# Attention and mixture-of-experts kernel on one core: the output projection as three fp32r products, with one normed macro tile, one probability buffer and five routing groups at the end

## The chip, the core and the metric

The kernel runs on one core of a Trainium2 chip. The metric is the device time of one execution in microseconds (us). A profiled execution comes with a trace; a span is the time from its first to its last instruction. The engines are named as the profile names them: PE is TensorE (matrix products; PEld is its loading of weights), DVE is VectorE, ACT is ScalarE, POOL is GpSimd, and SP issues most of the DMAs.

## What is computed

64 sequences of 64 tokens and 256 features go through a conditioned low-rank adapter, attention with a sink logit, and a mixture of 32 experts of which each token takes 4. Cut to what matters (`h` is the head count 16 on 4 key/value heads):

```python
def reference(x, cond, ...):
    x0 = relu(x @ (w_down * dg + db)) @ (w_up * ug + ub) + x     # per sequence
    qkv = rmsnorm(x0, attn_norm_w) @ qkv_w + qkv_b               # q: 16x64, k, v: 4x64
    q, k = rope(q), rope(k)
    logits = causal(q @ k.T / 8)
    attn = exp(logits - logaddexp(logsumexp(logits), sink))
    y = attn @ v                                                 # 1024 wide
    x2 = x0 + (y @ proj_w + proj_b)                              # the output projection
    h2 = rmsnorm(x2, ffn_norm_w)
    topv, topi = top_k(h2 @ gate_w + gate_b, 4); gw = softmax(topv)
    y2 = sum over the 4 experts e of gw_e * (silu(h2 @ Wg_e) * (h2 @ Wu_e)) @ Wd_e
    return x + x2 + y2
```

## The kernel before, in words

**Two parts.** The 4096 tokens are 8 macro tiles of 512 tokens (index m), each of 4 tiles of 128 tokens (index t, 0 to 31). Part one, the first 520 us or so, does adapter, attention, projection and routing. Part two runs some 159 expert tiles of 128 listed tokens each, then adds the four rows of every token. The change is in part one.

**Order.** Every engine runs a list of steps written out by hand in `ORDERS`: a start, a first period, a period that is repeated for each macro tile, and an end. The period of m does the attention and projection of macro tile m's tiles and, interleaved, the norm and the query/key products (`pair`, five of them) of macro tile m + 1. An engine waits at a step until semaphores say that its inputs and its output buffer are ready; steps behind it on that engine wait too.

**The chain of one tile.** `score` (PE) makes the logits in PSUM; `softmax_a` (DVE: a row maximum, L1497, and a subtraction, L1499), an exponential on ACT, and `softmax_b` (DVE: a sum, L1505, a reciprocal and the normed probabilities `prob`, L1516) follow; `turn_prob` (PE, L873) transposes them and ACT copies them out; `attend` (PE, L888) makes y in two PSUM banks; ACT copies y to `y_t` (L1186, two instructions per tile); `project` (PE) adds x0 and the product of `y_t` and `w_o` in one PSUM bank (L903); DVE adds the bias and writes `x2` (L1526). The product is in plain fp32: 8 products of 128 x 128 x 256 per tile, which the trace shows as 16 instructions.

**The norm of the next macro tile.** `sums` (PE, L811), two ACT instructions, `apply` (DVE: L1465 multiplies, ACT takes the upper part, L1469 subtracts it for the lower part). The two parts, `h_t`, feed the fp32r products of `pair` (PE, L822) and `value` (L834, six products each). An fp32r product here is three: upper by upper, upper by lower, lower by upper. `pair`'s results go through DVE (L1482, four of 128x512 per pair) and POOL (L708, L710), and are moved to `q_r` and `k_r` by DMAs that SP issues.

**Routing.** A group of tiles (`ROOTS`) is routed together: `route_turn` for each of its tiles (PE, ACT), `route_pick` (PE logits, DVE L1535 to L1563: the four best experts), `route_count` (PE, DVE), `route_list` (DVE L1583 to L1602: the slots). Then ACT packs and tags the rows (`pack`, `tag`) and POOL writes them to the experts' lists (`put`, L719, four indirect DMAs per tile). Before, the groups are the macro tiles 0 to 6 whole, and the last one as 2, 1 and 1 tiles: ten groups. When the last put has landed, ACT loads list rows (L1324) and part two begins, if the plan of expert tiles that DVE makes from the last counts (to L1710) is ready.

**Weights.** Between these steps each expert matrix is loaded, split by ACT (`split`, L1241) and POOL (L726) into two parts, and stored to `w_parts`.

## Time and profile before

| | |
|---|---|
| Times of three runs | 986.27, 989.08, 989.81 us; median 989.08 us |
| The profiled execution | 986.29 us, span 984.4 us |
| PE busy | 883.4 us (90%), 7248 instructions |
| PEld busy | 730.9 us (74%) |
| DVE busy | 793.0 us (81%), 1795 instructions |
| ACT busy | 523.8 us (53%) |
| POOL busy | 544.6 us (55%) |

The page's shares are means over both parts. For part one the stretches must be read apart: by the eight `apply` steps (L1465), which start at 31.4 us and then every 57 to 59 us from 78.7 to 426.8 us. A stretch's row gives the busy time of each engine in it. A busy PE is not PE at its peak, since the ends of its instructions are modelled and neighbours overlap; DVE's are as they ran.

### The profile page before, as it was taken

Reading aid. Unit: us, or ns where it says so; the run is one execution under the profiler, and the core shown is the slowest. Engines: PE = TensorE matmul, PEld = TensorE weight load, DVE = VectorE, ACT = ScalarE, POOL = GpSimd, SP = SyncE. Lnnn points to the kernel's source line nnn. Section 1 sums busy time; section 2 is a strip of 40 time slices with the busy share of each in tenths; the row PEclk is TensorE's granted clock in tenths of the full one; section 3 lists DMA queues with packets and bytes.
Section 4 is the critical chain, followed back from the end, with each engine's and each line's share of the span. In section 5 each row is a group of like instructions: output and inputs, shape, how many; then the busy total and the mean of one; then the engine's idle time right before and its main releaser. Section 6 shows DMA issues by size and latency. Waiting matters only on the chain.

```text
span 984.4 us, 21528 instructions
## 1 busy us (share of the span) xinstructions
PE 883.4 (90%) x7248; PEld 730.9 (74%) x7280; DVE 793.0 (81%) x1795; ACT 523.8 (53%) x1241; POOL 544.6 (55%) x507
## 2 busy tenths in 40 slices
PE   3759899898989989898981899999999999999998
PEld 1537677676767768676760688888888888888887
DVE  5888699899989989897764577777777787777777
ACT  3134464645647464563660466666666666666641
POOL 3455668888788888888357133343433333433340
PEclk8879999999999999999895799999999999999999
DMA  8388999888897988979239777877777758663698
GB/s 287 91 248 278 299 299 266 267 279 256 271 289 253 303 271 279 279 243 286 104 108 369 233 255 250 295 247 257 251 249 273 266 192 301 243 231 106 247 394 302
DMA packets 127446, 251.39 MB, mean 255 GB/s; under 512 B 18756, under 2 KB 66122, under 8 KB 126797
## 3 DMA queue, kind: packets, MB, share of 16 engines
q1 hardware_dynamic: 83436, 186.79, 57.4%
q0 software_dynamic: 13776, 34.64, 9.6%
q10 hardware_dynamic: 30128, 28.58, 9.4%
q8 instruction: 63, 1.03, 0.5%
q14 instruction: 43, 0.34, 0.1%
HBM read 135.64 MB, written 102.12 MB: 242 GB/s over the span
## 4 chain that ended last, share of the span: by engine, by line
PE 59%; DVE 11%; POOL 10%; issue 7%; DMA 6%; ACT 4%; SPq 2%; ACTq 0%; DVEq 0%; POOLq 0%
PE scores L1031 11%; PE gbank L1031 11%; PE scores L1050 6%; PE gbank L1050 5%; PE gbank L903 5%; POOL lists L719 4%; PE gbank L822 3%; DMA w_parts<-ring 3%; DVE ring L1482 3%; POOL ring L726 3%; PE gbank L1094 2%; PE scores L1005 2%; PE gbank L1005 2%; PE gbank L1040 2%; PE scores L1040 2%
## 5 line engine op out<-in xcount | busy, mean ns | idle before, releaser
L741 POOL DMA_INDIRECT pick_rows<-rows_out,pair_i x159 | 158.6, 998 | 261.8 <-ACT rows_out L1306 258.3
L726 POOL TENSOR_TENSOR ring<-ring 128x512 fp32r<-128x512 f32 x96 | 125.3, 1319 | 84.1 <-ACT ring L1241 83.9
L1031 PE MATMUL scores<-ring,in_part 128*128 x480 | 133.3, 414 | 1.2 <-DVE in_part L1722 1.2
L1031 PE MATMUL gbank<-ring,in_part 128*128 x474 | 129.8, 409 | 0.0
L822 PE MATMUL gbank<-h_t,w_qk 128*128 128x512 f32 x480 | 119.2, 403 | 4.2 <-issue 3.8
L719 POOL DMA_INDIRECT lists<-put_rows,slot_i x104 | 101.3, 974 | 34.0 <-issue 28.5
L903 PE MATMUL gbank<-w_o,ring 128*128 128x256 f32 x512 | 118.1, 385 | 1.3 <-ACT ring L1186 1.1
L1241 ACT ACTIVATE ring<-ring 128x512 fp32r<-128x512 f32 x96 | 58.9, 627 | 113.1 <-DMA w_parts<-ring 65.0
L1482 DVE SCALAR_TENSOR_TENSOR ring<-gbank,b_qk,rope 128x512 f32<-128x512 f32 x160 | 108.6, 743 | 6.6 <-PE gbank L822 4.2
L822 PEld LDWEIGHTS gbank<-h_t,w_qk 128*128 128x128 f32 x480 | 89.6, 191 | 28.4 <-issue 7.7
L903 PEld LDWEIGHTS gbank<-w_o,ring 128*128 128x128 f32 x512 | 96.2, 193 | 14.5 <-ACT ring L1186 2.6
L1031 PEld LDWEIGHTS scores<-ring,in_part 128*128 128x128 f32 x480 | 85.6, 192 | 15.9 <-issue 1.6
L1031 PEld LDWEIGHTS gbank<-ring,in_part 128*128 128x128 f32 x474 | 83.3, 189 | 13.7
L1050 PEld LDWEIGHTS scores<-ring,mid_part 128*128 128x128 f32 x480 | 67.8, 189 | 7.7 <-issue 0.4
L1050 PEld LDWEIGHTS gbank<-ring,mid_part 128*128 128x128 f32 x474 | 67.0, 189 | 7.2
L1292 ACT ACTIVATE in_part<-scores,norm_w 128x128 fp32r<-128x128 f32 x160 | 50.0, 364 | 39.5 <-PE scores L1005 22.0
L1050 PE MATMUL scores<-ring,mid_part 128*128 x480 | 70.1, 282 | 0.1
L1050 PE MATMUL gbank<-ring,mid_part 128*128 x474 | 69.2, 282 | 0.0
L1730 DVE SCALAR_TENSOR_TENSOR mid<-scores,rows_in,silu 128x256 f32<-128x256 f32 x80 | 38.6, 483 | 35.6 <-ACT silu L1298 35.6
L1298 ACT ACTIVATE silu<-scores,rows_in 128x256 f32<-128x256 f32 x80 | 37.9, 473 | 51.7 <-PE scores L1031 51.7
L1730 DVE SCALAR_TENSOR_TENSOR mid<-gbank,rows_in,silu 128x256 f32<-128x256 f32 x79 | 38.1, 482 | 27.0 <-ACT silu L1298 27.0
L1298 ACT ACTIVATE silu<-gbank,rows_in 128x256 f32<-128x256 f32 x79 | 37.4, 473 | 41.7 <-PE gbank L1031 40.8
(210 smaller groups left out, 1864.0 us busy)
## 6 DMA issues: line engine op xcount, KB each, us to landing
w_parts<-ring SPq DMA_DIRECT2D x192, 256.0 KB, 3.8
ring<-w_parts SPq DMA_DIRECT2D x32, 1536.0 KB, 7.7
rows_in<-lists ACTq DMA_DIRECT2D x159, 136.0 KB, 3.9
ring<-in_W_up SPq DMA_DIRECT2D x64, 256.0 KB, 3.7
picks<-pick_rows SPq DMA_DIRECT2D x6, 2048.0 KB, 17.9
ring<-in_W_down SPq DMA_DIRECT2D x32, 256.0 KB, 4.7
q_r<-rot SPq DMA_DIRECT2D x16, 512.0 KB, 6.4
q_r<-ring SPq DMA_DIRECT2D x16, 512.0 KB, 5.9
```

What stands on the lines that cost most here:

```text
L719: e.indirect_dma_start(out=lists, out_offset=bass.IndirectOffsetOnAxis(ap=slot_i[r % NPAY][:, s * TOPK + k:s * TOPK + k + 1], axis=0), in_ ...
L726: e.tensor_tensor(lower, lower.bitcast(F32), upper.bitcast(F32), ALU.subtract).then_inc(s_lower, 1)
L741: e.indirect_dma_start(out=pick_rows, out_offset=bass.IndirectOffsetOnAxis(ap=pair_i[:, i:i + 1], axis=0), in_=rows_out[i % NY][:, :], in_ ...
L822: ins = e.matmul(bank[:, :], w_qk[:, x, c, 2 * j + o, :], h_t[i][:, y, c, :], start=k == 0, stop=k == len(CHUNK_PRODUCTS) - 1)
L903: ins = e.matmul(bank[:, 0:D], y_t[:, n // REP, n % REP, :, :].rearrange("p b s -> p (b s)"), w_o[:, n, :], start=False, stop=n == 2 * REP ...
L1031: ins = e.matmul(front[i % FRONTS], in_parts[i % IN_BUFS][x][:, c, :], ring[:, bass.ds(at + y * WE + c * 2 * DFF, 2 * DFF)], start=k == 0, ...
L1050: ins = e.matmul(out, mid_parts[i % 2][x][:, c, :], ring[:, bass.ds(at + y * WE + KC * 2 * DFF + c * D, D)], start=k == 0, stop=k == len(C ...
L1241: e.activation(w_upper[q % NU], w_third[q % NW].bitcast(F32), ACT.Copy).then_inc(s_upper, 1)
L1292: ins = e.activation(in_parts[i % IN_BUFS][0][:, c, :], front[i % FRONTS][:, c * P:(c + 1) * P], ACT.Copy, scale=norm2_w[:, c:c + 1])
L1298: e.activation(silu[i % 2][:, :], front[i % FRONTS][:, DFF:2 * DFF], ACT.Silu, scale=rows_in[i % NG][:, D + 2:D + 3]).then_inc(s_silu, 1)
L1482: e.scalar_tensor_tensor(out=by_seq(t[n][:, :]), in0=by_seq(gbank[banks[o]][:, :]), scalar=b_qk[:, 2 * j + o:2 * j + o + 1], in1=rope[:, t ...
L1730: e.scalar_tensor_tensor(out=mid[i % MID_BUFS][:, :], in0=front[i % FRONTS][:, 0:DFF], scalar=rows_in[i % NG][:, D + 2:D + 3], in1=silu[i ...
```

## The change

- **Projection.** `w_o` becomes two fp32r parts, `w_o[0]` (upper) and `w_o[1]` (lower). They are made once by a new step `outs` (two ACT copies and two DVE subtractions of 128x1024; the matrix is loaded into `x2` first). `y_t` becomes two fp32r tiles: ACT's copy writes the upper part, and a new DVE step `attend` subtracts it from PSUM for the lower part, two instructions of 128x512 per tile. `project` makes 24 fp32r products instead of 8 in fp32. The two PSUM banks of y are freed by the DVE step and no longer by the ACT copy.
- **Buffers.** To make room, `h_t` is one macro tile instead of two (with `act` inside it), `prob` is one buffer instead of two, `x2_t` lies in the ring of expert weights (so those loads wait for the last routing product), and `v_s` has five buffers instead of two, since all four `value` steps of a macro tile now come before the next `down`.
- **Routing.** The last two macro tiles are routed in five groups (2, 2, 2, 1 and 1 tiles) instead of four (4, 2, 1 and 1). The four extra put buffers go to tiles 26 to 29 instead of 24 to 27.
- **Order.** All lists in `ORDERS` are new. A third entry of `SUMS` that was always 0 is removed with its code.

```diff
-SUMS = [(3, 1, 0), (3, 1, 0), (2, 2, 0), (3, 1, 0), (2, 2, 0), (2, 2, 0), (2, 2, 0), (3, 1, 0)]
+SUMS = [(3, 1), (3, 1), (2, 2), (3, 1), (2, 2), (2, 2), (2, 2), (3, 1)]
...
-        softmax_a softmax_a value softmax_b apply project softmax_b pair pair route_pick pair value
-        softmax_a route_count project pair pair value route_list softmax_b value down project relu
+        softmax_a softmax_a softmax_b attend apply project softmax_b pair pair route_pick pair
+        attend softmax_a project route_count pair pair value value value route_list value attend
...
-ROOTS = [(m, 0, TPM) for m in range(NM - 1)] + [(NM - 1, 0, 2), (NM - 1, 2, 3), (NM - 1, 3, 4)]
+ROOTS = [(m, 0, TPM) for m in range(NM - 2)] + [(NM - 2, 0, 2), (NM - 2, 2, 4), (NM - 1, 0, 2), (NM - 1, 2, 3),
+                                                (NM - 1, 3, 4)]
...
-    w_o = sb1("w_o", [P, H * DH // P, D])
+    w_o = [sb1(f"w_o{h}", [P, H * DH // P, D], F32R) for h in range(2)]
...
-    h_t = [sb1(f"h_t{i}", [P, 2, KC, MT], F32R) for i in range(2)]
+    h_t = sb1("h_t", [P, 2, KC, MT], F32R)
+    act = h_t[:, 0, 0, :]
...
+    y_t = [sb1(f"y_t{h}", [P, 2, REP, 2, T], F32R) for h in range(2)]
+    x2_t = ring_space[:, (NW + NU) * THIRD:(NW + NU) * THIRD + KC * TPM * P].rearrange("p (c n) -> p c n", c=KC)
...
-    prob = [sb1(f"prob{i}", [P, 16, T]) for i in range(2)]
+    prob = sb1("prob", [P, 16, T])
...
         w.wait_ge(s_proj, NT)
+        w.wait_ge(s_gate, GROUPS)
         for n in range(1, RING):
             load_expert(n)
...
             for b in range(2):
-                freed[banks[b]] = (s_y, 2 * t + b + 1)
+                freed[banks[b]] = (s_y_lower, 2 * t + b + 1)
...
             w.wait_ge(s_y, 2 * t + 2)
-            for n in range(2 * REP):
-                ins = e.matmul(bank[:, 0:D], y_t[:, n // REP, n % REP, :, :].rearrange("p b s -> p (b s)"), w_o[:, n, :],
-                               start=False, stop=n == 2 * REP - 1, skip_group_check=True)
+            w.wait_ge(s_o_split, 2)
+            for x, y in ((0, 0), (0, 1), (1, 0)):
+                if x:
+                    w.wait_ge(s_y_lower, 2 * t + 2)
+                for n in range(2 * REP):
+                    ins = e.matmul(bank[:, 0:D], y_t[x][:, n // REP, n % REP, :, :].rearrange("p b s -> p (b s)"),
+                                   w_o[y][:, n, :], start=False, stop=x == 1 and n == 2 * REP - 1, skip_group_check=True)
...
+        def outs():
+            w.wait_ge(s_late, LATE)
+            for h in range(2):
+                at = slice(h * REP, (h + 1) * REP)
+                e.activation(w_o[0][:, at, :], x2[h][:, :, :], ACT.Copy).then_inc(s_o_upper, 1)
...
+        def outs():
+            for h in range(2):
+                at = slice(h * REP, (h + 1) * REP)
+                w.wait_ge(s_o_upper, h + 1)
+                e.tensor_tensor(w_o[1][:, at, :], x2[h][:, :, :], w_o[0][:, at, :].bitcast(F32),
+                                ALU.subtract).then_inc(s_o_split, 1)
+
+        def attend(t, banks):
+            if t:
+                w.wait_ge(s_proj, t)
+            for b in range(2):
+                w.wait_ge(s_y, 2 * t + b + 1)
+                e.tensor_tensor(y_t[1][:, :, :, b, :].rearrange("p g j s -> p (g j) s"),
+                                gbank[banks[b]][:, :].rearrange("p (c s) -> p c s", s=T),
+                                y_t[0][:, :, :, b, :].rearrange("p g j s -> p (g j) s").bitcast(F32),
+                                ALU.subtract).then_inc(s_y_lower, 1)
...
-            if t >= 2:
-                w.wait_ge(s_pt, 2 * t - 2)
+            if t:
+                w.wait_ge(s_pt, 2 * t)
```

In the rows below, `beside` and `stat` hold a tile's row maxima and sums, `gbank` are PSUM banks and `glog` the routing logits.

On DVE, at the start of a period, before: from the second tile's `softmax_b` to the first `pair`.

```order
L1505 TENSOR_REDUCE beside1<-scores 128x16
L1508 TENSOR_REDUCE stat1<-beside1 128x16
L1510 RECIPROCAL stat1<-stat1 128x16
L1516 TENSOR_TENSOR prob1<-scores,stat1 128x1024
L1465 TENSOR_TENSOR ring<-x0_t1,gbank0 128x512 x2
L1469 TENSOR_TENSOR h_t1<-ring,h_t1 128x512 x2
L1526 TENSOR_TENSOR x2_0<-gbank2,b_o 128x256
```

And now, at the same place on DVE:

```order
L1523 TENSOR_REDUCE beside1<-scores 128x16
L1526 TENSOR_REDUCE stat1<-beside1 128x16
L1528 RECIPROCAL stat1<-stat1 128x16
L1534 TENSOR_TENSOR prob<-scores,stat1 128x1024
L1446 TENSOR_TENSOR y_t1<-gbank1,y_t0 128x8x64
L1446 TENSOR_TENSOR y_t1<-gbank2,y_t0 128x8x64
L1483 TENSOR_TENSOR ring<-x0_t1,gbank0 128x512 x2
L1487 TENSOR_TENSOR h_t<-ring,h_t 128x512 x2
L1544 TENSOR_TENSOR x2_0<-gbank3,b_o 128x256
```

Two subtractions (L1446) stand in front of `apply`; the same two are added for each of the four tiles of a period.

On DVE, in the end section, before: from the second `softmax_a` of tiles 29 and 30 to the pick of tiles 24 to 27.

```order
L1499 SCALAR_TENSOR_TENSOR scores<-beside0,scores 128x1024
L1505 TENSOR_REDUCE beside1<-scores 128x16
L1508 TENSOR_REDUCE stat1<-beside1 128x16
L1510 RECIPROCAL stat1<-stat1 128x16
L1516 TENSOR_TENSOR prob1<-scores,stat1 128x1024
L1491 TENSOR_TENSOR v_s1<-gbank2,b_v 128x256
L1505 TENSOR_REDUCE beside0<-scores 128x16
L1508 TENSOR_REDUCE stat0<-beside0 128x16
L1510 RECIPROCAL stat0<-stat0 128x16
L1516 TENSOR_TENSOR prob0<-scores,stat0 128x1024
L1526 TENSOR_TENSOR x2_1<-gbank3,b_o 128x256
L1535 TENSOR_TENSOR glog<-gbank2,rms2_0 128x128
```

And now, on DVE from the same `softmax_a`:

```order
L1517 SCALAR_TENSOR_TENSOR scores<-beside0,scores 128x1024
L1560 SCALAR_TENSOR_TENSOR glog<-gbank2,rms2_0,b_gate 128x32 x2
L1566 MAX top<-glog 128x8 x2
L1569 MAX_INDEX top_i<-top,glog 128x8 x2
L1570 TENSOR_TENSOR gexp<-top 128x8
L1573 TENSOR_TENSOR onehot<-expert_no,top_i 128x256
L1581 TENSOR_REDUCE picked<-onehot 128x64
L1446 TENSOR_TENSOR y_t1<-gbank3,y_t0 128x8x64
L1446 TENSOR_TENSOR y_t1<-gbank0,y_t0 128x8x64
```

The pick of tiles 24 and 25 has moved in front of two `softmax_b` steps, a `value` and a `project`.

## Rows read from the trace of the kernel before

**Rows 1.** The page, part 4: the chain that ended last, shares of the span.

```profile
PE 59%; DVE 11%; POOL 10%; issue 7%; DMA 6%; ACT 4%; SPq 2%; ACTq 0%; DVEq 0%; POOLq 0%
```

**Rows 2.** Busy time by stretch: from:to, length, each engine (instructions), PE clock, DMA share, GB/s.

```profile
78.69:426.83 348.14, 319.20 (x3381) 248.08 (x3404) 316.69 (x511) 192.83 (x424) 277.77 (x238) 1.00 0.87 277
426.83:476.00 49.17, 43.96 (x385) 34.77 (x387) 40.00 (x71) 21.92 (x50) 37.60 (x33) 0.93 0.78 243
476.00:521.00 45.00, 36.38 (x473) 28.18 (x474) 33.43 (x96) 30.56 (x80) 21.82 (x24) 0.97 0.36 122
546.00:984.40 438.40, 434.10 (x2662) 386.54 (x2660) 338.77 (x989) 255.24 (x649) 158.63 (x159) 0.99 0.74 257
```

**Rows 3.** Waits of DVE, 78.69 to 426.83: us in total, times, longest.

```profile
DVE beside L1497 <- PE scores L860: 6.2, 4, 2.1
DVE act L1396 <- ACT act L1116: 5.2, 6, 1.6
DVE gbank L1383 <- PE gbank L790: 2.7, 1, 2.7
DVE beside L1497 <- issue: 2.2, 2, 1.1
DVE v_s L1491 <- PE gbank L834: 1.8, 5, 1.1
...
DVE h_t L1469 <- ACT h_t L1163: 0.3, 1, 0.3
```

**Rows 4.** DVE subtractions and products by line: duration in ns, least/median/most; and one pair of them.

```profile
L1465 DVE TENSOR_TENSOR ring<-x_t,gbank x14: 679/685/689, 78.7 to 427.4; 128x512 f32<-128x512 f32 x14
L1595 DVE TENSOR_TENSOR onehot<-onehot,rank x10: 285/682/1829, 165.4 to 523.6; 128x512 f32<-128x512 f32 x7, 128x128 f32<-128x128 f32 x2, 128x256 f32<-128x256 f32 x1
369.60 1.28 DVE L1465 TENSOR_TENSOR ring<-x_t,gbank 128x512 f32<-128x512 f32 x2
```

**Rows 5.** The chain that ended last in order of time: start, us, what.

```profile
442.60 0.71 PE gbank L834 x6
...
443.53 3.46 PE gbank L903 x16
...
463.69 2.65 issue
...
470.55 5.42 PE gbank L903 x16
```

**Rows 6.** Timeline of POOL, the last 32 puts: start, us, [idle before, releaser].

```profile
500.29 0.95 POOL L719 DMA_INDIRECT lists<-q_r,slot_i  x1 [16.47 <-ACT q_r L1233]
...
539.62 0.96 POOL L719 DMA_INDIRECT lists<-q_r,slot_i  x1 [0.30 <-issue]
```

**Rows 7.** Timeline of DVE and of ACT's queue, end of part one.

```profile
482.35 1.22 DVE L1505 TENSOR_REDUCE beside<-scores 128x16 f32<-128x1024 f32 x1
...
489.62 0.29 DVE L1535 TENSOR_TENSOR glog<-gbank,rms 128x128 f32<-128x128 f32 x1 [0.47 <-PE gbank L925]
...
498.37 0.17 DVE L1602 CAST slot_i<-slot_f 128x16 int32<-128x16 f32 x1
...
524.26 0.17 DVE L1602 CAST slot_i<-slot_f 128x4 int32<-128x4 f32 x1
...
533.83 0.41 DVE L1710 TENSOR_SCALAR ring_wait<-x_t 1x32 int32<-1x32 f32 x1
...
542.15 3.74 ACTq L1324 DMA_DIRECT2D rows_in<-lists  x6
```

**Rows 8.** Timeline of the start, where `outs` goes.

```profile
26.00 2.88 DVE L1430 TENSOR_TENSOR w_qk<-q_r,w_qk 128x1280 fp32r<-128x1280 f32 x2
...
30.07 0.66 ACT L1154 ACTIVATE gbank<-gbank,eps 128x512 f32<-128x512 f32 x1 [3.33 <-PE gbank L811]
...
36.90 13.47 DVE L1482 SCALAR_TENSOR_TENSOR ring<-gbank,b_qk,rope 128x512 f32<-128x512 f32 x19 [2.52 <-PE gbank L822]
```

**Rows 9.** Busy time by stretch, just after the wait at 463.69 (columns as in rows 2).

```profile
466.00:476.00 10.00, 9.08 (x98) 6.71 (x100) 5.34 (x6) 3.79 (x9) 4.82 (x6) 0.66 0.51 186
```

More of the change, by code:

```diff
@@ L74 @@
     "PE": ("""
[L75 removed]
+        cond down up sums pair pair pair pair pair value value value value down score up
     """, """
[L77 to L79 removed]
+        score turn_prob sums attend score project pair pair turn_prob score attend pair project pair
@@ L89 @@
+        route_count turn_prob attend score route_pick project route_turn turn_prob route_count
+        route_turn route_pick attend project turn_prob route_count route_turn attend route_pick
+        project route_count route_turn route_pick route_count
     """),
     "DVE": ("""
-        cond down relu scale up weights apply pair pair pair pair pair constants down relu softmax_a
-        up softmax_b value
+        cond down relu scale up weights apply outs pair pair pair pair pair value value constants
@@ L93 @@
+        down value relu value softmax_a up softmax_b
     """, """
-        value softmax_a softmax_b apply project softmax_a pair pair softmax_a value pair softmax_b
-        project value pair pair softmax_b down relu project value softmax_a up softmax_b project
+        softmax_a softmax_b attend apply project softmax_a pair pair softmax_a attend pair softmax_b
+        project pair pair value value value value attend softmax_b project down softmax_a relu
+        attend up softmax_b project
@@ L457, in program @@
         sem(f"s_{n}") for n in ("summed", "tile_sum", "put_no", "put_wait"))
-    s_third_half, s_third_whole, s_third_sum = (sem(f"s_third_{n}") for n in ("half", "whole", "sum"))
     s_entry, s_top = sem("s_entry"), sem("s_top")
@@ L1502, in softmax_b @@
         def softmax_b(t):
[L1503 removed]
+            st, pr, two = stat[t % 2], prob, beside[t % 2]
             w.wait_ge(s_exp, t + 1)
```

188 lines of the change are left out of this document (86 added, 102 removed).

## The prediction

> **What bounds the kernel now.** I read the chain that ended last first, because it is the view that would recommend this change: 59% of it lies on PE [rows 1], and the projection is PE work. A chain names one engine at each moment and does not say how much room the next one has. So I read the busy time by stretch next. Part two (546 to 984 us) has PE busy for 434.10 of 438.40 us [rows 2], and none of its instructions change. In the six periods from 78.69 to 426.83 us PE is busy 319.20 and DVE 316.69 of 348.14 us [rows 2]: two engines side by side, and the change takes from one and gives to the other. The third view is therefore DVE's waits in those periods: ten kinds, of which the five largest (6.2, 5.2, 2.7, 2.2 and 1.8 us) and the smallest (0.3) are shown [rows 3]; all ten sum to 23.6 us. DVE takes 348.1 - 23.6 = 324.5 us for its own instructions and the gaps that belong to them. That is the number to hold the added work against: DVE has 23.6 us free in 348, and only if every wait vanishes. After 427 us it is looser: DVE is busy 40.00 of 49.17 and 33.43 of 45.00 us [rows 2]. There the end is set by something else: POOL stands idle for 16.47 us, then issues the last 32 puts without a pause from 500.29 to 540.58, one every 1.26 us [rows 6], and the first row loads follow at 542.15 [rows 7].
>
> **The change, part by part.**
>
> *PE, projection.* The 16 instructions of a tile take 3.46 us on the chain; six fp32r products of the same 256 columns take 0.71, so 0.118 each [rows 5]. 24 of them: 2.84 us. PE saves 0.62 us per tile, 15 us over the 24 tiles of the six periods and 20 over all 32. What of it reaches the end is decided by DVE.
>
> *DVE, the lower part of y.* 64 new instructions of 128x512 with one input in PSUM and one in SBUF. The nearest row is L1465, of the same shape and the same kinds of input: 0.685 us each, and two in a row take 1.28, so the second starts 0.60 after the first [rows 4]. The ends for one are 0.60 and 0.69 us; I take 0.65, as each waits for its own half of ACT's copy. A gain is excluded: the instruction is added to a queue that runs in order. Between the first and last of the seven `apply` steps stand the subtractions of 24 tiles: 48 x 0.65 = 31 us (28.8 to 32.9). L1595, with both inputs in SBUF, is as long as L1465 at its median, 0.682, but reached 1.829, while fourteen of L1465 stayed within 0.679 and 0.689 although POOL was busy 277.77 of 348.14 us [rows 2, 4]. The Trainium skill, GPSIMD Engine Reference, section 1 (Specifications), says that GpSimd shares its SBUF interfaces with VectorE and that contention comes with instructions in a two-port mode or with two SBUF inputs. The trace agrees with it for these two lines; were the new instructions stretched like the longest L1595, the sum by it would be 48 x 1.83 = 88 us in place of 31.
>
> *What the waits give back.* Waits for PE, those on the score step's issue among them, can shrink as PE gets lighter: 6.2 + 2.7 + 2.2 + 1.8 = 12.9 us [rows 3]. The 5.2 us before L1396 stay: `relu` still stands one short instruction behind `down`. Each `attend` step brings a new wait, for PE's y and ACT's copy. Mostly a `softmax_b`, a `route_list` or pairs lie between, which cover that chain; the ends are nothing and L1396's mean wait for ACT, 5.2 / 6 = 0.87, which is 21 us for 24. I take 4, near the lower end, because the steps ahead on DVE are longer than that chain. The six periods: 31 - 12.9 + 4 = **+22 us**. With every wait gone and no new one it is 28.8 - 23.6 = +5; with none gone and half the new ones 32.9 + 10 = +43.
>
> *ACT, POOL and SP.* ACT's copies are the same in number. POOL's and SP's lists hold the same steps in another order; POOL is busy 277.77 of 348.14 [rows 2], so 70 us of room hide that in the periods. Without this room POOL's pair steps would delay the moves and so the scores.
>
> *Single buffers.* `prob`: `softmax_b` now waits for the transpose of the tile before. It writes `prob` only after its sum (1.22 us [rows 7]), and PE has that transpose right behind the projection. `h_t`: the next `down` waits for four `value` steps, which are moved ahead for that. Both are covered in the periods by DVE's own queue; uncovered they would cost about one L873 or L834 step per tile. I put nothing here; the 4 us above cover it.
>
> *Start.* `outs` puts two ACT copies where ACT idles 3.33 us, and two DVE subtractions of 128x1024 where DVE idles 2.52 us before the first pair [rows 8]. L1430's two of 1280 columns take 2.88, so these take about 2.3. They need the late loads landed, some 17 DMAs that SP now issues earlier by three thirds' transfers. If those came late, the whole start would be pushed by the delay. The three `value` steps moved ahead fill an idle PE; tile 0's subtraction stands before the first `apply`. Together **+1** (-1 to +3).
>
> *426.83 to 476.* One tile's subtraction stands before the end of the last pairs: 1.3 us; two more fall into waits that this stretch has (9.17 us idle in 49.17, [rows 2]). **+1** (0 to +3).
>
> *The tail.* Before, two `softmax_b`, a `value` and a `project` stand on DVE from 482.35 to 489.62, 7.3 us, and pick, count and list of the four tiles 24 to 27, with what lies between them, take 8.9 us to the slots at 498.54 [rows 7]: 16.2 us. Now the pick of tiles 24 and 25 comes first, and one `softmax_b` (3 us, somewhat under half of the 7.3) and a subtraction step (1.3) stand between pick and list. The routing of two tiles costs between half of the 8.9 and all of it; I take 6, since each of its instructions has a fixed part. 6 + 3 + 1.3 = 10.3 us, with ends at 8.8 and 13.2. So the first put goes about 6 us earlier and, if POOL is fed from then on, the last one too. The floor is the plan: ready at 534.24, 9.98 us after the start of the last slots at 524.26 [rows 7], against 542.15; with eight more subtractions among the last four tiles' waits it comes 0 to 3 us later, which leaves 5 to 8 us. **-6** (-8 to 0). The loads of experts 1 to 3 now wait for the last routing product, some 7 us; expert 0's tiles cover that.
>
> *Sum.* 22 + 1 + 1 - 6 = +18 us. The profiled execution took 986.29 us (span 984.4 and 1.9 around it) and would become 1004. It is the fast end of three runs; the median, 989.08, is 2.8 above it. I forecast the median: **1007 us**.
>
> **The rivals.**
>
> *DVE's waits all vanish.* If the new order fits DVE without a hole, the periods cost +5 and the tail gives 6 to 8 back: about 989, no change. For it: PE gets lighter by 15 us. Against it: the 5.2 us at `relu`, whose place is kept, and the chain of POOL and a DMA that the score step waits for, which no lighter PE shortens.
>
> *PE is the bound: faster.* The mechanism is that the chain's 59% on PE is what sets a period, so that 0.62 us per tile comes off it: -15 in the periods, -6 in the tail, 968 us. It decides if an added subtraction costs DVE less than 23.6 / 48 = 0.49 us, the point at which the waits hold them all; L1465's lowest spacing is 0.60 [rows 4]. PE's busy share in the periods is 92%, but its weight loading is 248.08 of 348.14, 71%, against DVE's 91% [rows 2]. The Trainium skill, Perfetto Trace Analysis, section Identifying the Most-Contended Engine, says that matmul busy time is a bad measure of TensorE's load, that the share of LDWEIGHTS is a good one, and that for VectorE occupancy is. By that rule DVE is the contended engine and relief on PE returns nothing, so the sum stays +22 in the periods; by the matmul share it would be -15. The rule speaks against this change.
>
> *PE's clock falls.* When PE stood still for 2.65 us at 463.69, the stretch behind it ran at a granted clock of 0.66, part of it at 1.2 instead of 2.4 GHz, and the projection took 5.42 in place of 3.46 us [rows 5, 9]. A PE that now waits for DVE could fall like that once per period: 2 us on the projection, 12 in six periods: 1019. Against it: in the periods the granted clock was 1.00 [rows 2], with PE waits in them.
>
> *The change doesn't do what it says.* If the 24 products ran no faster than the 16 instructions (0.144 each), PE would save nothing and both engines would stay full; waits would not shrink by 12.9: 1020. The row of 0.118 speaks against it.
>
> **How the numbers follow.** Forecast 1007: 0.66. Waits vanish, 989: 0.12. Faster, 968: 0.05. Clock, 1019: 0.12. No saving on PE, 1020: 0.05. About 0.5%, 5 us, is what a measurement of this kernel can tell from no change, so "same" is 984 to 994. Faster holds the PE rival, 0.05; same holds the vanished waits and the lowest of the forecast's own range (+5 in the periods), 0.13; slower the rest, 0.82. The range goes from 991 (periods at about +6) to 1022 (periods at +37, or the clock); below it lie most of "same" and "faster", some 0.13, above it 0.06.
>
> **What would show it.** Right: periods of 60 to 62 us between `apply` steps instead of 57.2 to 59; DVE busy above 94% of them; its waits below 17 us with the one before `relu` among the largest; PE's matmul share down to about 84%; the projection at 2.8 us in 24 instructions; each new subtraction 0.68 us long; the first put of tiles 24 and 25 about 10 us after the pair of `softmax_a`, and puts that end some 6 us sooner behind the last `softmax_a`. Wrong: periods of 58 us with DVE at 97% (waits vanished), shorter periods with idle DVE (PE was the bound), granted clocks below 1 in the periods, or subtractions of over 1 us.

## The result, and the profile after

The changed kernel takes 1012.31 us (median; 1010.53 to 1014.17) where the kernel before, measured beside it on the same chip, takes 987.67 (median of four): the ratio is 1.0246, with an interval of 1.0203 to 1.0289. The profiled execution spans 1008.4 us against 984.4. The forecast was 1007, in a range of 991 to 1022.

The chain that ended last has moved from PE towards DVE (59% and 11% in [rows 1]); the page's part 4 of the kernel after:

```profile
PE 55%; DVE 16%; POOL 9%; DMA 7%; issue 6%; ACT 5%; SPq 2%; ACTq 0%; DVEq 0%; POOLq 0%
```

The eight `apply` steps (now L1483) start at 31.84, 81.00, 143.89, 204.73, 264.64, 324.83, 385.95 and 446.61 us. Busy time by stretch answers to [rows 2], with the same columns (from:to, length, PE, PEld, DVE, ACT, POOL, PE clock, DMA share, GB/s):

```profile
81.00:446.61 365.61, 319.72 (x3598) 249.39 (x3597) 339.08 (x561) 191.62 (x422) 278.31 (x236) 0.98 0.83 263
...
570.00:1008.40 438.40, 433.58 (x2660) 385.90 (x2658) 337.14 (x983) 252.88 (x645) 158.65 (x159) 0.99 0.74 256
```

The six periods take 365.61 us in place of 348.14. DVE is busy 92.7% of them (91% before). PE is busy 319.72 us, and the row of before says 319.20, although the projections have become lighter by some 13 us (24 tiles, 3.62 us before and 3.08 after). Part of this is the trace: it lacks one of the two mask products of every `score` before, while it has all weight loads (six periods, before and after):

```profile
L850 PEld LDWEIGHTS scores<-mask,mask_rows x48: 95/98/102, 87.9 to 418.1; 128*128 128x128 bf16 x48
L850 PE MATMUL scores<-mask,mask_rows x24: 378/379/380, 88.1 to 418.3; 128*128 128x512 bf16 x24
L836 PE MATMUL scores<-mask,mask_rows x48: 377/379/391, 89.8 to 437.7; 128*128 128x512 bf16 x48
```

The 48 take 14.4 us of PE's busy time and the 24 take 9.1, so PE was busy some 324.5 us before (an estimate from these two) and is busy about 5 us less now.

Waits of DVE in the six periods, all seven kinds, against [rows 3]:

```profile
DVE y_t L1446 <- ACT y_t L1184: 6.2, 1, 6.2
DVE beside L1515 <- PE scores L846: 3.4, 4, 1.6
DVE x L1544 <- PE gbank L893: 3.2, 4, 1.3
DVE h_t L1397 <- ACT h_t L1107: 2.2, 5, 0.4
DVE v_s L1509 <- PE gbank L820: 1.5, 1, 1.5
DVE v_s L1509 <- PE gbank L874: 0.9, 1, 0.9
DVE ring L1500 <- PE gbank L808: 0.5, 1, 0.5
```

They sum to 17.9 us (23.6 before), and only 8.5 of it are of kinds that the kernel before had; the first and the third line, 9.4 us, are new. So DVE takes 365.6 - 17.9 = 347.7 us for itself, 23.2 more than before. Its groups by line in that stretch (count, busy us, mean ns, then idle before) say from what. The new subtraction, and the two small routing instructions that changed most, before:

```profile
L1592 DVE TENSOR_TENSOR entry<-gexp,gsum 128x16 f32<-128x16 f32 x5 | 9.9, 1985 | 0.4
...
L1595 DVE TENSOR_TENSOR onehot<-onehot,rank 128x512 f32<-128x512 f32 x5 | 6.8, 1365 | 0.0
```

and after:

```profile
L1446 DVE TENSOR_TENSOR y_t<-gbank,y_t 128x512 fp32r<-128x512 f32 x49 | 31.5, 684 | 6.4 <-ACT y_t L1184 6.2
...
L1613 DVE TENSOR_TENSOR onehot<-onehot,rank 128x512 f32<-128x512 f32 x5 | 4.5, 908 | 0.0
...
L1610 DVE TENSOR_TENSOR entry<-gexp,gsum 128x16 f32<-128x16 f32 x5 | 2.5, 492 | 0.4
```

PE's waits have grown: 28.0 us in the six periods before, 44.4 after. The largest of after:

```profile
PE gbank L893 <- ACT y_t L1184: 10.9, 6, 1.8
PE gbank L885 <- DVE ring L1500: 8.3, 5, 2.3
PE scores L846 <- issue: 6.4, 5, 2.2
PE gbank L787 <- DVE y_t L1446: 6.4, 5, 1.4
```

The first is the projection waiting for ACT's copy of y, once per period, 1.8 us each. The timeline of PE shows one of them, a later projection of the same macro tile, and a projection of the kernel before (start, us, what, [idle before]):

```profile
263.53 4.63 PE L893 MATMUL gbank<-w_o,y_t 128*128 128x256 f32 x24 [1.82 <-ACT y_t L1184]
...
299.00 3.08 PE L893 MATMUL gbank<-w_o,y_t 128*128 128x256 f32 x24
...
153.06 3.62 PE L903 MATMUL gbank<-w_o,ring 128*128 128x256 f32 x16
```

Why the first takes 4.63 us is in the stretches of 1.5 us around it:

```profile
261.00:262.50 1.50, 0.70 (x10) 0.20 (x2) 1.33 (x4) 1.47 (x4) 1.20 (x2) 1.00 0.93 237
262.50:264.00 1.50, 0.47 (x3) 0.47 (x4) 1.50 (x2) 0.98 (x3) 1.32 (x2) 0.93 0.99 367
264.00:265.50 1.50, 1.50 (x9) 1.50 (x9) 1.50 (x4) 0.15 (x1) 1.19 (x2) 0.50 0.61 221
265.50:267.00 1.50, 1.50 (x9) 1.50 (x9) 1.40 (x3) 1.50 (x3) 1.20 (x2) 0.50 0.95 280
267.00:268.50 1.50, 1.50 (x14) 1.50 (x14) 0.61 (x2) 0.84 (x3) 1.20 (x2) 0.93 0.83 317
```

The granted clock falls to 0.50 (1.2 GHz) right behind the wait. Read so, in stretches of 1.5 us, the clock falls four times in the six periods after, and once before. PE's busy time in each stretch, times the part of the clock that is missing, sums to 6.7 us after and 1.7 before; this is called the clock's share below.

The end of part one: POOL's puts, against [rows 6] (the first of the last 32, the one behind the only long hole, the last):

```profile
514.35 0.95 POOL L716 DMA_INDIRECT lists<-put_rows,slot_i  x1 [6.06 <-ACT put_rows L1232]
...
523.27 0.96 POOL L716 DMA_INDIRECT lists<-put_rows,slot_i  x1 [4.17 <-ACT put_rows L1232]
...
557.70 0.96 POOL L716 DMA_INDIRECT lists<-put_rows,slot_i  x1 [0.30 <-issue]
```

The first row loads, on ACT's queue, follow at 563.68; the last rows of x2 and the loads of experts 0 to 3 on SP's queue stand in the second fence:

```profile
563.68 4.02 ACTq L1325 DMA_DIRECT2D rows_in<-lists  x6
```

```profile
532.81 7.60 SPq L528 DMA_DIRECT2D x_rows<-x  x2
540.73 9.49 SPq L603 DMA_DIRECT2D ring<-w_parts  x4
```

Counted from the last `apply`, the first late put has come 5.7 us forward (67.74 us, 73.46 before), the last put's end 1.7 us (112.05, 113.75), the row loads have gone 1.8 us back (117.07, 115.32), and the first expert product 2.0 us back (122.79, 120.75).

### The profile page after: what moved, and what is told of

Read it like the earlier page. It is cut to its first block, busy times and chain, and to the rows that moved or that the text cites. A ratio compares the mean times of both kernels' runs of the same rounds, so it can differ in the third digit from the quotient of the medians.

```text
span 1008.4 us, 22157 instructions
## 1 busy us (share of the span) xinstructions
PE 884.8 (88%) x7537; PEld 733.5 (73%) x7537; DVE 831.2 (82%) x1874; ACT 524.7 (52%) x1248; POOL 545.3 (54%) x506
## 4 chain that ended last, share of the span: by engine, by line
PE 55%; DVE 16%; POOL 9%; DMA 7%; issue 6%; ACT 5%; SPq 2%; ACTq 0%; DVEq 0%; POOLq 0%
PE scores L1021 11%; PE gbank L1021 10%; PE scores L1040 5%; PE gbank L1040 5%; PE gbank L893 4%; DVE ring L1500 4%; POOL lists L716 4%; PE gbank L808 3%; DMA rows_in<-lists 2%; PE gbank L1084 2%; PE scores L995 2%; PE gbank L995 2%; PE gbank L1030 2%; PE scores L1030 2%; DVE y_t L1446 2%
## 5 line engine op out<-in xcount | busy, mean ns | idle before, releaser
L716 POOL DMA_INDIRECT lists<-put_rows,slot_i x112 | 108.2, 966 | 57.5 <-ACT put_rows L1232 29.0
L893 PE MATMUL gbank<-w_o,y_t 128*128 128x256 f32 x768 | 107.4, 298 | 15.2 <-ACT y_t L1184 14.3
L893 PEld LDWEIGHTS gbank<-w_o,y_t 128*128 128x128 f32 x768 | 100.3, 202 | 19.0 <-ACT y_t L1184 17.1
```

The costliest lines, as they stand in the source:

```text
L716: e.indirect_dma_start(out=lists, out_offset=bass.IndirectOffsetOnAxis(ap=slot_i[r % NPAY][:, s * TOPK + k:s * TOPK + k + 1], axis=0), in_ ...
L893: ins = e.matmul(bank[:, 0:D], y_t[x][:, n // REP, n % REP, :, :].rearrange("p b s -> p (b s)"), w_o[y][:, n, :], start=False, stop=x == 1 ...
```

## The experiments

The question was whether the added subtractions are what the periods have grown by. "Six periods" is the time from the second to the eighth `apply` of the profiled execution.

| run | order of the steps | projection | subtraction | us, median | ratio to before, interval | six periods, us |
|---|---|---|---|---|---|---|
| before | old | 16, fp32 | none | 987.67 | | 348.1 |
| old_24 | old | 24, fp32r | none | 992.78 | 1.0020 (0.9991 to 1.0050) | 358.4 |
| old_sub | old | 16, fp32 | once | 1028.47 | 1.0367 (1.0307 to 1.0426) | 388.2 |
| old_both | old | 24, fp32r | once | 1016.77 | 1.0258 (1.0204 to 1.0311) | 376.4 |
| fp32_order | new | 16, fp32 | none | 1011.33 | 1.0248 (1.0192 to 1.0304) | 369.8 |
| order_buffers | new, two buffers | 16, fp32 | none | 1011.32 | 1.0222 (1.0172 to 1.0272) | 368.7 |
| no_sub | new | 24, fp32r | none | 1003.97 | 1.0142 (1.0092 to 1.0192) | 367.2 |
| products_16 | new | 16, fp32r | once | 1008.87 | 1.0223 (1.0172 to 1.0275) | 369.2 |
| after | new | 24, fp32r | once | 1012.31 | 1.0246 (1.0203 to 1.0289) | 365.6 |
| double_sub | new | 24, fp32r | twice | 1035.75 | 1.0488 (1.0419 to 1.0557) | 388.8 |

Each ratio is to the kernel before as it ran beside that run (medians of 987.67 to 990.99 us), so runs are best compared by their ratios. The six periods come from one execution of each, and it is not always a typical one: it was the slowest of its run in old_24 (4.7 us above the median), old_both (4.1), old_sub (3.0) and no_sub (2.3), and the fastest in order_buffers (6.2 below), fp32_order (4.4) and after (1.8). A difference of some 5 us in the last column can come from that.

**no_sub.**

```diff
-    softmax_a softmax_a softmax_b attend apply project softmax_b ...
+    softmax_a softmax_a softmax_b apply project softmax_b ...
...
-                freed[banks[b]] = (s_y_lower, 2 * t + b + 1)
+                freed[banks[b]] = (s_y, 2 * t + b + 1)
...
-            for x, y in ((0, 0), (0, 1), (1, 0)):
+            for last, x, y in ((0, 0, 0), (0, 0, 1), (1, 0, 1)):
```

> Leaves out the lower part of y: the DVE step attend is gone from every list, the PSUM banks of y are freed by ACT's copy, and the third product takes y's upper part and the lower weights a second time, so that PE issues the same 24 products per tile. Theory (DVE sets the periods): its 48 subtractions at 0.60 us leave the six periods, 28.8 us; waits grow by some of that, so the periods fall from 365.6 to 342 to 348 us, and the time by 18 to 26 us, to 986 to 994. Rival (PE, or the wait of the projection for a longer chain of y, sets them): PE's work is the same, the time stays within 5 us of 1012.

The time fell by 8 us, not by 18 to 26, and the six periods of the profiled execution did not fall at all (367.2). The stretch, the largest waits of DVE, and of PE:

```profile
77.54:444.73 367.19, 320.52 (x3613) 255.13 (x3603) 312.42 (x513) 191.26 (x423) 279.71 (x235) 0.96 0.83 263
```

```profile
DVE x L1542 <- PE gbank L891: 19.1, 8, 9.0
DVE h_t L1395 <- ACT h_t L1105: 6.4, 5, 1.4
DVE beside L1521 <- ACT scores L1164: 5.7, 3, 1.9
```

```profile
PE gbank L885 <- DVE ring L1498: 11.3, 5, 3.3
PE gbank L891 <- ACT y_t L1182: 9.1, 5, 1.8
PE gbank L797 <- ACT ring L1199: 6.6, 5, 2.1
```

DVE's 26.7 us of work less became waits (46.2 us in all, 19.1 of them for PE's projection; 17.9 in the kernel after), while PE waited 44.6 us, for a bank that DVE's `pair` frees and for ACT's copies. The clock falls seven times, and its share is 14.1 us instead of 6.7, so part of what DVE gave back went there. What its profiled execution is shorter by (4.3 us of span) lies outside the periods: the second `apply` comes 3.5 us earlier, and from the last one to the first expert product it is 2.4 us less. My theory, that DVE sets the periods of the new order, falls in this form.

**products_16.**

```diff
-            for x, y in ((0, 0), (0, 1), (1, 0)):
+            for x, y in ((0, 0), (1, 0)):
```

> Leaves out one of the three products (y's upper part by the weights' lower part): 16 fp32r products per tile on PE instead of 24, nothing else. PE loses 8 x 0.118 = 0.94 us per tile, 22.7 us in the six periods. Theory (DVE sets the periods): they stay at 60 to 61 us, at most 4 us of the 22.7 come back as shorter waits, the time is 1006 to 1012. Rival (PE is the bound): the periods fall by 15 to 22 us, the time to 985 to 995.

The six periods did not get shorter (369.2, a little above the 360 to 366 expected), and the time lies in the theory's range. But PE's busy time fell by 7.3 us and not by 22.7:

```profile
79.02:448.18 369.16, 312.38 (x3404) 237.76 (x3403) 341.71 (x561) 191.67 (x422) 278.85 (x236) 0.94 0.82 261
```

The clock falls eleven times here and its share is 22.1 us. A third of the projection less returns nothing clear of noise in this kernel; what it would return at the full clock is not shown.

**double_sub**, in `attend` on DVE.

```diff
-            for b in range(2):
-                w.wait_ge(s_y, 2 * t + b + 1)
+            for n in range(2):
+                for b in range(2):
+                    w.wait_ge(s_y, 2 * t + b + 1)
...
+                    if n:
+                        ins.then_inc(s_y_lower, 1)
```

> Each of the 64 subtractions for y's lower part is made twice on DVE, into the same place; PE, ACT and POOL as after the change. 48 more instructions of 0.60 to 0.68 us in the six periods, 29 to 33 us, of which the remaining 17.9 us of DVE's waits can take some. Theory (DVE sets the periods): they grow by 20 to 32 us, DVE's share rises above 95%, the time is 1034 to 1050. Rival (DVE has room, and the 20 us of the change come from the order of the steps or from the single buffers): the time grows by less than 10 us.

The periods grew by 23.2 us, the time by 23; DVE's share rose to 94.3%, not above 95%. The second set of subtractions costs nearly its own length; the first, by no_sub, cost nothing in the periods of this order that one execution of each can show.

**fp32_order**: DVE's lists as in no_sub, and

```diff
-    y_t = [sb1(f"y_t{h}", [P, 2, REP, 2, T], F32R) for h in range(2)]
+    y_t = [sb1(f"y_t{h}", [P, 2, REP, 2, T], (F32, F32R)[h]) for h in range(2)]
...
-            for x, y in ((0, 0), (0, 1), (1, 0)):
+            for x, y in ((0, 0),):
```

and the same for `w_o`.

> The new order, the single buffers, the five routing groups, but the projection in one plain fp32 product per tile as before the change: no subtraction on DVE, y and the weights in one part (the lists of DVE without attend; outs stays at the start). Theory (the added DVE work is the cost, the order and the buffers cost little): the six periods come back to 343 to 350 us, and the time to 983 to 992. Rival (the new order with one normed macro tile and one prob buffer costs by itself): the periods stay above 354 us and the time above 997.

The rival held: with the work of the kernel before, the new order takes 1011 us, as much as the whole change. The clock's share is 9.9 us in its six periods, 1.7 in the kernel before; the periods are 22 us longer.

**order_buffers.**

```diff
-    h_t = sb1("h_t", [P, 2, KC, MT], F32R)
+    h_t = [sb1(f"h_t{i}", [P, 2, KC, MT], F32R) for i in range(2)]
...
-    prob = sb1("prob", [P, 16, T])
+    prob = [sb1(f"prob{i}", [P, 16, T]) for i in range(2)]
```

> As fp32_order (the new order and five routing groups, plain fp32 projection, no subtraction for y), but with two normed macro tiles and two prob buffers again, in the room that the second parts of y and of the projection's weights took; outs makes one part only. fp32_order took 1011 us with its six periods at 369.8, although DVE had 45 us of waits in them. Theory 1 (the single buffers make the engines wait for each other): the six periods come back to 345 to 355 us, the time to 985 to 997. Theory 2 (the order of the steps does it, whatever the buffers): the periods stay at 362 to 370 us, the time at 1004 to 1012.

Theory 2: two buffers change nothing (368.7 against 369.8). What the new order costs does not lie in the buffers' waits. The five routing groups alone do not make it either (old_five below: six periods of 349.0 us). That leaves the order of the steps, with the place of `x2_t` and the five `v_s` buffers, which were not tried alone.

**old_sub, old_24, old_both.** In the old order; the subtraction (old_sub, old_both) is

```diff
+            for b in range(2):
+                y = gbank[banks[b]][:, :].rearrange("p (c s) -> p c s", s=T)
+                w.wait_ge(s_y, 2 * t + b + 1)
+                e.tensor_tensor(y, y, y_t[:, :, :, b, :].rearrange("p g j s -> p (g j) s").bitcast(F32),
+                                ALU.subtract).then_inc(s_y_lower, 1)
```

and the projection (old_24, old_both), whose extra products start sums of their own in the bank that collects x2, so that x2, and with it the choice of experts in part two, is not the reference's there,

```diff
+            for k in range(3):
...
+                    ins = e.matmul(bank[:, 0:D] if k == 2 else bank[:, D:2 * D],
...
+                                   start=k < 2 and n == 0, stop=n == 2 * REP - 1, skip_group_check=True)
```

> The kernel before with nothing but the 64 subtractions on DVE, two per tile, put in its lists where the change has them; their result goes back into the PSUM bank and is not used, and the banks of y are freed by them. PE, the order otherwise and all buffers as before. 48 x 0.60 to 0.68 us are 29 to 33 us in the six periods against 23.6 us of waits of DVE there. Theory 1 (the added DVE work is the cost, whatever the order): the periods grow by 12 to 24 us, the time is 1000 to 1012. Theory 2 (most of the cost of the change is the new order or the single buffers, since taking the subtraction out of it gave only 8 us back): they grow by 5 to 12 us, the time is 993 to 1001.

> The kernel before with its projection as 24 fp32r products per tile of 3.08 us in place of 16 fp32 instructions of 3.62 us; only one part of y and of the weights exists, two thirds of the products go to columns of the PSUM bank that nobody reads. No subtraction, the order as before; the transposed rows of the routing lie in the ring, so the loads of experts 1 to 3 wait for the last routing product. Theory 1 (DVE sets the periods, lighter PE work returns nothing): the periods stay within 5 us of 348, the time at 983 to 990. Rival (PE sets them): 24 x 0.55 = 13 us less, 968 to 976.

> old_sub and old_24 together: the change's PE work and DVE work in the old order with the old buffers (the results of the subtraction and of two thirds of the products are not used). Theory 1 (the work is the cost): like the change, periods of 360 to 367 us together, 1003 to 1013 us. Theory 2 (the new order and the single buffers are most of the cost): periods of 350 to 358, 989 to 1000 us; then the difference to 1012 us is what order and buffers cost.

Neither theory on old_sub went far enough: its periods grew by 40 us for 29 us of work (the places of the steps in the old lists are mine, and new waits came with them; the clock's share is 13.0 us, 11 more than before). old_24 refutes its rival: by the medians its time is the same (1.0020, an interval that holds 1). In its profiled execution, the slowest of ten, the periods are 10 us longer, although PE's work is lighter by 13 us. The clock there is 0.96 where it was 1.00 [rows 2], its share 13.1 us, about what the projections saved:

```profile
78.19:436.57 358.38, 319.06 (x3597) 249.89 (x3596) 317.18 (x512) 192.32 (x424) 278.99 (x238) 0.96 0.85 270
```

The clock falls seven times in it, each time where PE stood still for 2.1 us or more. One, in the timeline of PE and in stretches of 1.5 us:

```profile
236.91 1.98 PE L860 MATMUL scores<-k_r,q_r 64*64 64x64 f32 x64 [2.48 <-issue]
238.64 1.86 PE L888 MATMUL gbank<-ring,v_s 64*64 64x256 f32 x16
```

```profile
235.50:237.00 1.50, 0.09 (x4) 0.12 (x8) 0.72 (x2) 0.36 (x1) 1.20 (x2) 0.95 0.92 327
237.00:238.50 1.50, 1.50 (x60) 1.50 (x64) 0.00 (x0) 0.00 (x0) 1.20 (x2) 0.50 0.92 295
```

old_both is nearer to theory 1 and above its ranges (1016.77 us, periods of 376.4): in the old order the change's work costs as much time as the change did (1.0258 and 1.0246). Its six periods are 10.8 us longer than those of the kernel after, but the one execution is the slowest of its run and the other the fastest; by the medians the two kernels differ by 1.2 us, and their intervals overlap. That the new order gains anything for this work is not shown.

**fill.**

```diff
+            if t % TPM == 0 and t:
+                for _ in range(15):
+                    e.matmul(bank[:, D:2 * D], w_qk[:, 0, 0, 0, :], w_qk[:, 0, 0, 0:2, :].rearrange("p a n -> p (a n)"),
+                             start=True, stop=True, skip_group_check=True)
             w.wait_ge(s_y, 2 * t + 2)
```

(These products, too, start their own sums in the bank of x2, which is not the reference's.)

> The changed kernel with 15 more fp32r products (128 x 128 x 256, of weights that lie still, into columns of the bank that nobody reads) in front of the first projection of each macro tile from the second on, where PE stands still for 1.8 us until ACT has copied y. In the trace of the changed kernel the granted clock falls to 0.50 for 3 to 4 us right behind such a wait, in three of the six periods from 81 to 447 us, and the projection takes 4.3 to 4.6 us in place of 3.1. Theory (the wait lets the clock fall, and the fall costs time): with PE busy there, none of these three falls is left, those projections take 3.1 us, the mean clock of the stretch is 0.99 or more, and the time falls by 3 to 7 us, to 1005 to 1009. Rival (the falls have another cause, or lie off the path): they stay, or go and the time stays at 1010 to 1016, or rises by the 1.8 us per macro tile where there was no wait.

1007.82 us, ratio 1.0196 (1.0151 to 1.0242). PE's timeline at one of the places, L889 being the fillers, and the clock there:

```profile
255.28 2.03 PE L889 MATMUL gbank<-w_qk 128*128 128x256 f32 x15
257.36 3.10 PE L897 MATMUL gbank<-w_o,y_t 128*128 128x256 f32 x24
```

```profile
256.50:258.00 1.50, 1.45 (x12) 1.25 (x11) 1.50 (x3) 0.80 (x2) 1.33 (x2) 1.00 0.83 276
258.00:259.50 1.50, 1.50 (x15) 1.50 (x15) 1.50 (x3) 0.33 (x1) 1.20 (x2) 1.00 0.69 253
```

All six first projections of a macro tile take 3.1 us and the three falls are gone: with PE busy in the wait of 1.8 us the clock does not fall there. Three falls came at other places (338, 361 and 427 us), so the mean clock stayed 0.98 and the clock's share is 6.4 us, hardly less than 6.7. The time fell by 4.5 us, as expected, but its interval overlaps that of the kernel after: that the wait brings the fall is shown at these three places, the gain is not settled.

**tag_loads, old_five, old_five_early**, for the end of part one. The edits in turn: on ACT

```diff
-        route_pick pack pack turn_prob pack tag attend pack pack route_turn turn_prob tag project
+        route_pick pack pack turn_prob pack tag tag attend pack pack route_turn turn_prob project
```

and on SP

```diff
         w.wait_ge(s_proj, NT)
-        w.wait_ge(s_gate, GROUPS)
-        for n in range(1, RING):
+        for n in range(2, RING):
             load_expert(n)
+        w.wait_ge(s_gate, GROUPS)
+        load_expert(1)
```

then the five groups alone in the old order (on DVE shown)

```diff
-        softmax_a softmax_a softmax_b value softmax_b project route_pick value project route_count
+        softmax_a softmax_a route_pick softmax_b value route_count route_list softmax_b project
```

and, on top of that, on SP

```diff
+                if k == NT - 3:
+                    load_early()
                 store_x2(k)
```

> The changed kernel with two moves at the end of part one: on ACT the second tag of tiles 24 to 27 stands right behind the first, in front of a copy of y and two packs; on SP the loads of experts 2 and 3 no longer wait for the last routing product, only that of expert 1 does, in whose slot the transposed rows lie. Theory: POOL's hole of 4.17 us in the last 32 puts closes, the last put ends some 4 us earlier than 112.05 us after the last apply; the last put's rows land in about 2.5 us again in place of 5.9, as no three loads of 1.5 MB start beside them; together 5 to 8 us, the time 1004 to 1008. Rival: the later of the plan and the puts takes over, or the landing is long for another reason; then the hole closes, but the time falls by less than 4 us.

> The kernel before with nothing but the five routing groups of the change: tiles 24 and 25 are picked, counted and listed in front of the two last steps of softmax_b, tiles 26 and 27 behind them, tags and packs on ACT in that order. The periods stay as they are (348 us for six). Theory (what the change gained at the end came from the earlier first put, and nothing else in it is needed for that): the first of the last 32 puts goes 4 to 6 us earlier than 73.46 us after the last apply, the last one ends 3 to 6 us earlier than 113.75, and the time is 982 to 986, 0.3 to 0.6% under the kernel before. Rival (POOL runs dry between the groups, or the plan ends last): the time stays within 2 us of the kernel before.

> old_five with one more move: the loads of experts 0 and 2 (1.5 MB each) go out in front of the third last store of x2 on SP, at about 480 us, instead of behind the last one at 516.6; their ring slots hold nothing of part one any more, and the DMA engines stand idle from 485 to 490 us. In old_five the first late put went 8.3 us earlier than in the kernel before and the last one ended 4.0 us earlier, but the first row loads came only 0.8 us earlier, since the last put took 4.8 us to land in place of 1.6 while the DMA share was 0.96 to 1.02 from 525 to 540 us by four expert loads. Theory (those loads hold the last puts up): with two of them gone early, the traffic ends before 530 us, the last put lands in about 2 us, the row loads come some 3 us earlier than in old_five, and the time is 984 to 988, below old_five by 3 us and below the kernel before by 0 to 5. Rival (the put's landing or the plan is late for another reason): the row loads stay at 114 to 115 us after the last apply, the time at 989 to 993.

| from the last `apply`, us | last put ends | row loads | first expert product | part two from there | us, median; ratio |
|---|---|---|---|---|---|
| before | 113.75 | 115.32 | 120.75 | 436.8 | 987.67 |
| after | 112.05 | 117.07 | 122.79 | 439.0 | 1012.31; 1.0246 |
| tag_loads | 110.30 | 115.63 | 121.13 | 437.8 | 1009.72; 1.0200 (1.0151 to 1.0249) |
| old_five | 109.73 | 114.53 | 119.96 | 439.4 | 991.21; 1.0036 (1.0006 to 1.0066) |
| old_five_early | 110.10 | 111.67 | 117.10 | 439.0 | 990.16; 1.0001 (0.9971 to 1.0031) |

tag_loads was a miss on the landing: the last put still took 5.3 us to land, since all four loads stand behind the last store of x2 on SP, whatever they wait for; 1.4 us came forward at the row loads. old_five gained 4.0 us at the last put and 0.8 at the row loads. In old_five_early two loads go out at 491.5 us:

```profile
537.08 0.96 POOL L725 DMA_INDIRECT lists<-q_r,slot_i  x1 [0.30 <-issue]
```

```profile
539.61 3.73 ACTq L1330 DMA_DIRECT2D rows_in<-lists  x6
```

The last put lands in 1.57 us, as in the kernel before, and the first expert product comes 3.7 us earlier than there. That expert loads hold up the last puts is shown by this. The total is still that of the kernel before: part two took 2.2 us longer, with waits of PE for list rows in it. Over the eleven profiled executions other than old_24, old_both and fill, whose experts can be others, part two takes 436.8 to 439.4 us, and the kernel before had the shortest. No version was found that beats the kernel before.

## Why the prediction was right, and where not

The sum of the prediction against the spans: periods +22 forecast, +17.5 measured; start +1, +2.3 (81.00 against 78.69); the rest of part one +1 - 6 = -5, +2.0; part two 0, +2.2 (it varies by 2.6 from run to run). Together +18 and +24.0. The time is forecast well, and in part by luck: the prediction puts all of the growth on DVE's added work and nothing on the new order, and fp32_order shows that the new order alone, without that work, takes as long (1.0248 against 1.0246). In the new order the lighter projection then took some 10 us off (no_sub, 1.0142; the two intervals just touch), and the subtraction put as much on again.

- **The subtraction's price** was right: 684 ns, 0.60 between the starts of two, so 28.8 us at the low end of what was taken (31). It was not stretched beside POOL (672 to 702 ns). But DVE's own time grew by 23.2 only: L1592 and L1595 (now L1610 and L1613) lost 9.7 us, two other small routing instructions gained some 4. This term was left out. It goes with the order: L1592's five instructions took 5.2 us or more in every run of the old order, 2.5 in every run of the new one.
- **The waits** came out by compensation. Of the 12.9 us that were to go, 5.8 stayed (3.4 at the score step, 2.4 at `value`) and 7.1 went. Another 8.0 went from waits that were to stay: the one at `relu`, 5.2, is 2.2, and of the other kinds 0.5 is left of 5.5. The new waits, put at 4, are 9.4: 6.2 in one wait of the first period, 3.2 in front of x2. So 23.2 - 15.1 + 9.4 = 17.5 in place of 31 - 12.9 + 4 = 22.
- **ACT and SP** were put at nothing, and this term was missed. The wait of 6.2 us comes from ACT's new list: its step `split` stood for a matrix of an expert, with the copy of y behind it:

```profile
114.80 0.63 ACT L1240 ACTIVATE ring<-ring 128x512 fp32r<-128x512 f32 x1 [9.11 <-DMA ring<-in_W_down]
116.34 1.29 DVE L1446 TENSOR_TENSOR y_t<-gbank,y_t 128x512 fp32r<-128x512 f32 x2 [6.19 <-ACT y_t L1184]
```

  PE stood still for 5.69 us there and POOL for 4.80. Every run of the new order has this wait of ACT (6.5 to 9.1 us). ACT's waits in front of `split` sum to about the same before and after (92.6 and 87.6 us in six periods), but 46 have become 27 longer ones. Those for one kind of matrix, before and after:

```profile
ACT ring L1241 <- DMA ring<-in_W_up: 11.8, 7, 2.7
ACT ring L1240 <- DMA ring<-in_W_up: 37.4, 9, 6.9
```

- **PE's saving** came as 0.54 us per tile and not 0.62: 24 products take 3.08 us and not 2.84. What it returned cannot be read from the periods: PE's waits grew from 28.0 to 44.4 us. By the ratios, lighter work on PE returned nothing from before to old_24 and from after to products_16, and some 10 us from fp32_order to no_sub and from old_sub to old_both (1.0367 and 1.0258). The 84% forecast for its share is 87%. Four falls of the clock stretch what is left (6.7 us, 1.7 before), and the 319.20 us that the forecast started from were about 5 too low, as the missing mask products show. The rival on the clock has thus happened in part, beside the forecast and not in its place. The rival on PE as the bound, with its 968 us, is refuted by the result; that PE's work counts for nothing is not shown.
- **The tail** is the term that failed: -6, and the end came 2 us later. The first put moved as forecast (-5.7 us). "If POOL is fed from then on" did not hold: the second tag stood on ACT behind a copy of y and two packs, a hole of 4.17 us. And the loads of experts, costed only as a delay that expert 0's tiles cover, were the price: the last store of x2 and with it the four loads come 6.3 us later from the last `apply`, so they run into the last puts, which land in 5.0 us in place of 1.6.
- **The signs.** Periods of 60 to 62 us came (60.9 on average), and subtractions of 0.68 us. DVE above 94% (92.7%), waits below 17 us (17.9) and a projection of 2.8 us (3.08) did not, and a granted clock below 1 (0.98), named as a sign of being wrong, did.
- **The picture behind the sum** was too simple. It treats DVE's work as what fills a period. In the old order the change's work does cost about what was forecast (28 us in the six periods of old_both, 26 in its time). In the new order the periods last 363 to 370 us with the subtraction and without it, with 24 light, 16 heavy or 16 light products, with one buffer or two, and grow only when DVE gets a second set. There, engines wait for each other in turn. Why the order alone costs some 24 us in time is not shown: the lower clock, which takes 8 us more of PE's time in fp32_order, and ACT's longer waits for matrices of the experts are two candidates, and neither was taken out by a run.
- **The Trainium skill**, Perfetto Trace Analysis, section Identifying the Most-Contended Engine, judges TensorE by the share of LDWEIGHTS and VectorE by occupancy, and says to optimize the most contended engine first. By these measures that is DVE here (92.7%, against 249.39 of 365.61 us, 68%, of weight loading). The runs do not agree among themselves on that: products_16 and old_24 got nothing from lighter work on PE, old_both and no_sub some 10 us. And no_sub shows that taking 26.7 us from the engine so named can return nothing in the periods and 8 us in the time.

## What to carry to other kernels

Where two engines are both some 91% busy, work moved from one to the other is not paid by the difference of two sums: here the one that got lighter waited more, and PE, where it waited, was granted a lower clock, so the saved work can come back as nothing (old_24) or in part (old_both). Price a new order of the steps by itself, by running it with the old work (fp32_order): here it cost as much as the whole change. And hold a trace against the median of its runs before a difference of a few us is read from it (old_24, old_both). At a seam between two parts, follow the DMA traffic as well as the last instruction: a transfer that is issued later can hold up the one that the next part waits for.

## What the runs showed of the hardware that was not expected

- Behind, or in, waits of PE of 1.8 us and more the granted clock fell to 0.50 for 3 to 4 us, in some periods and not in others: of the six waits of 1.8 us in front of a projection in the kernel after, three were followed by a fall. tag_loads has the same instructions as the kernel after up to 446 us and shows eight falls in its six periods (368.4 us) where that shows four (365.6).
- Of the DVE instructions with both inputs in SBUF, small ones stretched most. One of 128x16 elements (L1592) took 1985 ns on average in the six periods before and 492 after; at 496.83 us of the kernel before, where POOL stood idle, it took 190. One of 128x128 took 290 ns at 489.95 us there, with POOL idle too. The same one in the kernel after,

```profile
458.08 5.36 DVE L1556 TENSOR_TENSOR glog<-glog,b_gate 128x128 f32<-128x128 f32 x1
```

  ended when POOL had finished a run of products without a pause between 455.82 and 463.29 us, which suggests POOL as the cause and does not prove it. The prediction had looked only at the new instruction, which has one input in PSUM and was never stretched (680 to 690 ns on average in the kernel after, double_sub, old_sub and old_both).
